# Attention with its side work in other places: the order of TensorE, VectorE, ScalarE and the loads around it

## The chip, the core and the metric

One Trainium2 chip, one of its cores. A core has TensorE (PE, matmul; its weight loads are the profile's PEld), VectorE (DVE), ScalarE (ACT), GpSimd (POOL) and SyncE (SP), which here only issues DMAs. The engines run their own instruction lists in order and wait for each other by semaphores. The metric is the time of one execution of the whole program on the device, in microseconds; lower is better.

## The reference

A decoder layer in float32 with batch 8, 224 tokens, width 512. Three parts, each with a layernorm ahead and a residual behind:

```python
x = x + mamba(layernorm(x))             # selective state space; ends with y @ W_out
x = x + cross_attention(layernorm(x), ctx)
x = x + moe(layernorm(x))               # router, 2 of 4 experts

qh = (q @ Wq + bq)   # 16 heads of 32; k and v from ctx (750 tokens) likewise
attn = softmax(qh @ kh.T / sqrt(32));  out = (attn @ vh) @ Wo + bo
router_logits = gelu(x @ rW1 + rb1) @ rW2 + rb2
```

## The kernel before

The program has four stages, one behind the other: `mamba_in`, `state_space`, `attention` and `experts`. Only `attention` is touched. Its input `y_d` (the state space's result), the keys `kh_d`, `kl_d` (high and low part) and the values `v_d` lie in device memory. It also computes what stands directly around the attention: the last projection of the mamba part (`project`), both layernorms (w = 0 for the attention, w = 1 for the experts), the queries, the end projection, and the router's hidden layer and logits.

The loop `steps()` runs over iterations `it` from -1 to 9 and, in each, over 16 slots `sl`, one per head; s = 16 it + sl is the head step. In a slot TensorE computes the scores of one head of one batch in two halves of 112 query rows, `scores(s, 0)` and `scores(s, 1)`. Both halves use the same two PSUM banks, so each one waits until VectorE has taken the row maxima of the half before (`negative_max`, a reduction over 750 keys, `max_done`). So a slot has two gaps for TensorE: one behind `scores(s, 0)` and one behind `scores(s, 1)`. In the first it computes the transposed scores of head s-3 (`turned_scores`), whose exponentials ScalarE then takes (`exponentials`) and GpSimd sums (`row_sum`). Every fourth slot has `values` (the product with v) and the next one `row_sums`, which waits for GpSimd's sums of four heads; every second slot has `turn_max`, which transposes the maxima for ScalarE's `turned_max`.

All other matmuls are side work. Iteration `it` prepares batch a = it+1 (project, layernorm w = 0, queries), finishes batch c = it-1 (end projection, layernorm w = 1, router's hidden layer) and has the logits of batch it-2. Slots 0 to 3 have one half of a projection each, slot 4 the logits, 5 and 6 the end projections, 8 both transposed norms, 9 to 12 the queries and the hidden layer, and 13 to 15 the rest of it. The whole order is written out by hand, in one loop per engine.

GpSimd's `with_bias(a)` in slot 10 writes x + bo into the buffer `xb[:, a % 2]`. It waits until the output of batch a-2 = c has been stored from the same buffer:

```python
if b >= 2:
    pool.wait_ge(x2_stored, 16 * (b - 1))
```

Next behind it in GpSimd's list stands the `row_sum` of that slot. SyncE stores that output in slot 8. It issues every DMA of the stage, all on one queue: keys for four heads in every slot with sl % 4 == 2, values in every slot with sl % 4 == 0, and the queries, which go to device memory and come back for a whole batch (`store_queries`, `load_queries`).

Iteration -1 has no head step: it is a prelude that only prepares batch 0. Iterations 8 and 9 drain the stage.

Of the kernel before, what the change touches and what calls it, by code (L numbers as in the profile page):

```python
# [13 lines left out]
P = 128  # L14
# [828 lines left out]
def attention(nc, x, kh_d, kl_d, v_d, y_d, W_out, Wq, bq, bv, Wo, bo, rW1, rb1, rW2, rb2, ident_in,  # L843
# [4 lines left out]

    ctx = ExitStack()
# [7 lines left out]
    with ctx:  # L857
# [3 lines left out]
        def sem(name):  # L861
# [29 lines left out]
        first_loaded, w_loaded, rest_loaded, g_loaded, x_loaded, q_loaded = (  # L891
            sem(n) for n in ("first_loaded", "w_loaded", "rest_loaded", "g_loaded", "x_loaded", "q_loaded"))
# [12 lines left out]
        N_W, N_REST = 4, 6  # L905
# [16 lines left out]
        def _(sp):  # L922
# [51 lines left out]
            load_g(1)  # L974
            for dst, src in ((bor[:], bo.partition_broadcast(P)), (wo[:], rows(Wo)), (rb1c[:], rb1), (rw1[:], rows(rW1)),
                             (rw2[:], rows(rW2)), (rb2r[:], rb2.partition_broadcast(P))):
                sp.dma_start(dst, src).then_inc(rest_loaded, 16)
            for j in range(KC):
                load_values(j)
            for it, sl, s in steps():  # L980
# [5 lines left out]
                if sl == 4 and it >= 0 and among(a + 1, B):  # L986
# [6 lines left out]
                if 9 <= sl < 9 + KC and among(a, B):  # L993
                    store_queries(a, sl - 9)
                if sl == 13 and among(a, B):
                    load_queries(a)
                    if a == 0:
                        load_keys(1)
                    if a + 1 < B:
                        load_x(a + 1)  # L1000
# [7 lines left out]
        def _(pool):  # L1008
# [15 lines left out]
            def with_bias(b):  # L1024
                if b == 0:
                    pool.wait_ge(rest_loaded, 16 * N_REST)
# [14 lines left out]
        def _(dve):  # L1041
# [16 lines left out]
            def statistics(b, w):  # L1058
                rows, ready = (xt, x1_done) if w == 0 else (xb[:, b % 2], x2_done)
                for u in range(2):  # L1060
                    dve.wait_ge(ready, 2 * b + u + 1)
                    nc.vector.bn_stats(st[:, 2 * w + u], rows[:, u]).then_inc(stat[w], 1)
# [6 lines left out]
            def normalise(b, w):  # L1069
                rows = xt if w == 0 else xb[:, b % 2]  # L1070
                dve.wait_ge(std[w], b + 1)
                nc.vector.reciprocal(rstd[:, w], rstd[:, w]).then_inc(rstd_done[w], 1)
                dve.wait_ge(rstd_done[w], b + 1)
                if b >= 1:
                    dve.wait_ge(xn_mm[w], 2 * b)
                    if w == 1:
                        dve.wait_ge(xn_stored, 16 * b)
                for u in range(2):
                    nc.vector.tensor_scalar(xn[w][:, u], rows[:, u], mv[:, 2 * w + u, 0:1], rstd[:, w, u:u + 1],
                                            ALU.subtract, ALU.mult).then_inc(xn_done[w], 1)  # L1080
# [9 lines left out]
            def hidden(b, q, bank):  # L1090
# [3 lines left out]
                nc.vector.tensor_scalar(rh[:, q], ps[:, bank, 0:L], rb1c[:, q:q + 1], None, ALU.add).then_inc(rh_pre, 1)  # L1094
# [5 lines left out]

            def outputs(J):
                b, j = J // KC, J % KC
                dve.wait_ge(sums_mm, J + 1)
                nc.vector.reciprocal(rinv[:], ps[:, PV_BANK, L:2 * L]).then_inc(rinv_done, 1)
                dve.wait_ge(rinv_done, J + 1)
# [12 lines left out]
            for it, sl, s in steps():  # L1118
                a, c, last = it + 1, it - 1, it - 2
                if it == 0 and sl == 0:  # L1120
                    dve.wait_ge(rest_loaded, 16 * N_REST)
                if among(s, STEPS):
                    negative_max(s, 0)
                if among(a, B):
                    if sl in (1, 3):
                        residual1(a, sl // 2)
                    if sl == 4:
                        statistics(a, 0)
                    if sl == 7:
                        normalise(a, 0)  # L1130
                    if 9 <= sl < 9 + KC:
                        low_queries(a, sl - 9)
                if sl == 4 and among(last, B):
                    logits(last)
                if among(c, B):
                    if sl in (5, 6):
                        residual2(c, sl - 5)
                    if sl == 6:
                        statistics(c, 1)
                    if sl == 7:  # L1140
                        normalise(c, 1)
                    if sl in (13, 14, 15):
                        hidden(c, {13: 4, 14: 6, 15: 7}[sl], BANK6)
                if among(s, STEPS):
                    negative_max(s, 1)
                if (s - SUM_LAG) % 4 == 0 and among((s - SUM_LAG) // 4, B * KC):
                    outputs((s - SUM_LAG) // 4)
                if among(c, B) and 9 <= sl < 14:
                    hidden(c, {9: 0, 10: 1, 11: 2, 12: 3, 13: 5}[sl], BANK5)

        @block.scalar
        def _(act):
# [19 lines left out]
            def turned_norm(b, w, u):  # L1172
                act.wait_ge(xn_mm[w], 2 * b + u + 1)
                nc.scalar.activation(xnT[w][:, :, u * TT:(u + 1) * TT],
                                     ps[:, (BANK6, BANK5)[u], 0:KC * TT].rearrange("p (k t) -> p k t", k=KC),
# [18 lines left out]
            for it, sl, s in steps():  # L1194
# [5 lines left out]
                if sl == 7:  # L1200
# [4 lines left out]
                if sl == 8:  # L1205
                    for w, b in ((0, a), (1, c)):
                        if among(b, B):
                            for u in range(2):
                                turned_norm(b, w, u)
                if 9 <= sl < 9 + KC and among(a, B):  # L1210
                    high_queries(a, sl - 9)
                if s % 2 == 0 and among((s - 2) // 2, STEPS // 2):
                    turned_max((s - 2) // 2)

        @block.tensor
        def _(pe):
# [60 lines left out]
            def project(b, u, half):  # L1277

                if half == 0:
# [6 lines left out]
                for c in range(4 * half, 4 * half + 4):  # L1286
                    ins = nc.tensor.matmul(ps[0:TT, (BANK5, BANK6)[u]], gT[:, c, u * TT:(u + 1) * TT], wout[:, c],
                                           start=(c == 0), stop=(c == CC - 1))
                if half == 1:
                    ins.then_inc(out_mm, 1)  # L1290

            def turn_norm(b, w, u):
                pe.wait_ge(xn_done[w], 2 * b + u + 1)
                if w == 0:
                    if b >= 2:
                        pe.wait_ge(x2_done, 2 * batches(b - 1))
                else:
                    pe.wait_ge(xn_turned[0], 2 * batches(b + 3))
                for k in range(KC):
                    ins = nc.tensor.transpose(ps[:, (BANK6, BANK5)[u], k * TT:(k + 1) * TT], xn[w][:, u, k * P:(k + 1) * P],  # L1300
# [3 lines left out]
            def queries(b, j):  # L1304
                if j == 0:
# [3 lines left out]
                    if b >= 2:  # L1309
                        pe.wait_ge(xn_turned[1], 2 * batches(b - 1))  # L1310
# [7 lines left out]
            def end_project(b, u):  # L1318
                if u == 0:
# [4 lines left out]
                elif b >= 1:  # L1324
                    pe.wait_ge(lg_done, 2 * batches(b))
                for j in range(KC):
                    ins = nc.tensor.matmul(ps[0:TT, (BANK6, BANK5)[u]], oT[:, j, u * TT:(u + 1) * TT], wo[:, j],
                                           start=(j == 0), stop=(j == KC - 1))
                ins.then_inc(wo_mm, 1)

            def hidden(b, q, bank):
                if q == 0:
                    pe.wait_ge(xn_turned[1], 2 * b + 2)
                elif q == 4:
# [539 lines left out]
```

## Time and profile before

| | us |
|---|---|
| median of 3 runs (lowest, highest) | 2938.28 (2930.95, 2944.82) |
| profiled execution, time / span | 2944.2 / 2942.5 |
| busy share of the span: PE, DVE, ACT, POOL | 85%, 49%, 41%, 44% |
| mean granted TensorE clock | 0.915 of full |
| attention: first DMA issue of the stage | 1078.6 |
| attention: first scores (iteration 0, slot 0) | 1153.57 |
| attention: iteration 1, slot 0 / iteration 7, slot 0 | 1241.26 / 1870.49 |
| attention: first DMA issue of the experts | 2021.65 |

Times of the trace count from the start of the span. The page cuts the span in 40 slices of 73.6 us each, and the attention fills slices 15 to 27:

```profile
PE   5998569999999974788988988883589989999991
PEclk9998779999999997799989999886799999999996
```

Each digit is a share in tenths: of busy time for PE, of full speed for PEclk, the clock that TensorE was granted. Nowhere in the attention's middle does PE reach the 99 of the neighbouring stages.

### The profile page before, as it was taken

How to read it: one execution, taken by the hardware profiler on the slowest of the kernel's cores; microseconds unless marked ns; L12 is line 12 of the kernel's file. 1: busy time of each engine (PE TensorE's matmuls, PEld its weight loads, DVE VectorE, ACT ScalarE, POOL GpSimd, SP SyncE). 2: the span in 40 equal slices, each digit the busy share in tenths (PEclk: the TensorE clock that was granted, in tenths of full speed). 3: DMA queues.
4: the chain of work that ended last, by engine and by line, in shares of the span. 5: the costliest groups of instructions: out<-in, count | busy, mean ns of one | idle time of the engine just before them, and what ended most of it. 6: DMA issues, size and time to landing. Idle time of an engine off the chain costs nothing. (4 is left out here: it accounts for less than half of the span.)

```text
span 2942.5 us, 39312 instructions
## 1 busy us (share of the span) xinstructions
PE 2491.5 (85%) x14320; PEld 2017.7 (69%) x14320; DVE 1430.8 (49%) x1880; ACT 1206.3 (41%) x2611; POOL 1297.2 (44%) x892
## 2 busy tenths in 40 slices
PE   5998569999999974788988988883589989999991
PEld 4984358888888862555665665652478888888881
DVE  5342479999999961455554454443021212121213
ACT  2333367777777621333433333332233333333330
POOL 3321247777777740544544544542563090009004
PEclk9998779999999997799989999886799999999996
DMA  9323765555565445434434452415531031002015
GB/s 290 126 105 95 222 192 170 164 160 157 175 172 175 133 137 133 114 93 104 113 95 94 106 119 70 108 29 187 179 107 57 29 122 42 15 29 79 29 64 157
DMA packets 257561, 349.20 MB, mean 119 GB/s; under 512 B 36574, under 2 KB 183966, under 8 KB 256270
## 3 DMA queue, kind: packets, MB, share of 16 engines
q1 hardware_dynamic: 235790, 281.32, 34.5%
q0 software_dynamic: 16256, 55.85, 5.7%
q10 hardware_dynamic: 5376, 10.23, 0.9%
q8 instruction: 81, 1.33, 0.2%
q14 instruction: 58, 0.48, 0.1%
HBM read 215.97 MB, written 131.35 MB: 118 GB/s over the span
## 5 line engine op out<-in xcount | busy, mean ns | idle before, releaser
L655 POOL TENSOR_TENSOR s_hc<-s_h,s_Cc 128x896 f32<-128x896 f32 x256 | 494.9, 1938 | 206.7 <-DVE s_h L760 102.4
L760 DVE TENSOR_TENSOR_SCAN s_h<-s_decay,s_ub 128x928 f32<-128x928 f32 x256 | 527.6, 2080 | 11.1 <-ACT s_decay L690 2.7
L798 PE MATMUL s_yps<-s_hc,s_ident 128*128 128x224 f32 x2048 | 431.1, 354 | 1.1 <-POOL s_hc L655 1.1
L1016 POOL TENSOR_TENSOR t_part<-t_pT 125x672 f32<-125x672 f32 x128 | 206.0, 1609 | 437.4 <-ACT t_pT L1159 437.0
L690 ACT ACTIVATE s_decay<-s_dt,s_A 128x224 f32<-128x224 f32 x1024 | 388.0, 470 | 18.4 <-DVE s_h L760 18.3
L1698 DVE TENSOR_TENSOR e_hl<-e_ps,e_hh 128x256 fp32r<-128x256 f32 x256 | 108.7, 425 | 573.0 <-ACT e_ps L1744 573.0
L798 PEld LDWEIGHTS s_yps<-s_hc,s_ident 128*128 128x128 f32 x2048 | 369.3, 191 | 2.0 <-POOL s_hc L655 1.4
L1046 DVE TENSOR_REDUCE t_nmax<-t_ps 112x1 f32<-112x752 f32 x256 | 239.8, 937 | 184.7 <-PE t_ps L1227 184.3
L1770 PE MATMUL e_ps<-e_xTh,e_w1h 128*128 128x256 f32 x1024 | 293.3, 286 | 23.5 <-DVE e_xTl L1690 23.5
L1159 ACT ACTIVATE t_pT<-t_ps 125x448 f32<-125x448 f32 x384 | 181.2, 545 | 317.8 <-PE t_ps L1251 306.5
L1743 ACT ACTIVATE e_hh<-e_ps,e_b 128x256 fp32r<-128x256 f32 x256 | 121.8, 476 | 421.9 <-PE e_ps L1772 421.7
L1771 PE MATMUL e_ps<-e_xTl,e_w1h 128*128 128x256 f32 x1024 | 292.9, 286 | 0.0
L1772 PE MATMUL e_ps<-e_xTh,e_w1l 128*128 128x256 f32 x1024 | 289.9, 283 | 0.0
L1227 PE MATMUL t_ps<-t_k,t_q 96*112 96x376 f32 x512 | 182.4, 440 | 104.8 <-DVE t_nmax L1046 78.9
L787 PE MATMUL s_ub<-s_diag,s_ut 96*128 96x224 f32 (+2 forms) x1024 | 232.3, 350 | 36.4 <-DVE s_diag L724 22.9
L787 PEld LDWEIGHTS s_ub<-s_diag,s_ut 96*128 96x128 f32 x1024 | 157.9, 194 | 107.0 <-issue 54.5
L1770 PEld LDWEIGHTS e_ps<-e_xTh,e_w1h 128*128 128x128 f32 x1024 | 197.2, 193 | 34.5 <-issue 24.6
L1770 PE MATMUL e_ps<-e_w2h,e_hh 128*128 128x512 f32 x512 | 205.1, 400 | 10.9 <-DVE e_hl L1698 10.9
L1568 POOL TENSOR_TENSOR e_w1h<-e_stage,e_one 128x2048 fp32r<-128x2048 f32 x12 | 43.3, 3607 | 386.0 <-PE e_ps L1772 385.8
L1771 PEld LDWEIGHTS e_ps<-e_xTl,e_w1h 128*128 128x128 f32 x1024 | 197.1, 192 | 9.2
L1772 PE MATMUL e_ps<-e_w2h,e_hl 128*128 128x512 f32 x512 | 201.6, 394 | 0.0
L1771 PE MATMUL e_ps<-e_w2l,e_hh 128*128 128x512 f32 x512 | 201.1, 393 | 0.0
(202 smaller groups left out, 4375.1 us busy)
## 6 DMA issues: line engine op xcount, KB each, us to landing
s_ut<-ut_d SPq DMA_DIRECT2D x192, 128.0 KB, 3.3
e_stage<-in_L_ffn_We POOLq DMA_DIRECT2D x24, 1024.0 KB, 5.6
t_k<-kh_d SPq DMA_DIRECT2D x64, 375.0 KB, 6.5
xs_d<-a_zero POOLq DMA_DIRECT2D x30, 512.0 KB, 12.5
s_Cc<-cs_d SPq DMA_DIRECT2D x8, 1792.0 KB, 9.6
kh_d<-s_kh SPq DMA_DIRECT2D x32, 375.0 KB, 2.7
kl_d<-s_kl SPq DMA_DIRECT2D x32, 375.0 KB, 2.8
v_d<-s_v SPq DMA_DIRECT2D x48, 250.0 KB
```

The costliest lines, as they stand in the source:

```text
L655: nc.gpsimd.tensor_tensor(hc[:, u % 2, k], h[:, u % 2, k, :, 2:SLOT], Cc[:, b % 2, k], ALU.mult).then_inc(hc_done, 1)
L690: ins = nc.scalar.activation(decay[:, u % 2, :, n, 2:SLOT], dts[:, u % 2].rearrange("p (s t) -> p s t", s=NSEG), ACT.Exp, scale=A[:, u % C ...
L760: nc.vector.tensor_tensor_scan(h[:, u % 2, k].rearrange("p n t -> p (n t)"), decay[:, u % 2, k].rearrange("p n t -> p (n t)"), ub[:, s % 2 ...
L787: ins = nc.tensor.matmul(at[:, first:end, half * FA:half * FA + width], ut[:, u // 2 % 2, 2 * k + half, u % 2 * P:u % 2 * P + P], diag[:, ...
L798: ins = nc.tensor.matmul(yps[:, u % 2, 0:L], ident[:], hc[:, u % 2, :, n], start=(n == 0), stop=(n == NS - 1))
L1016: nc.gpsimd.tensor_tensor(part[:], p[:, 0:3], p[:, 3:6], ALU.add).then_inc(sum_step, 1)
L1046: nc.vector.tensor_reduce(nmax[:, u, h:h + 1], ps[0:TT, 0:2, 0:EVEN], AX.XY, ALU.max, negate=True).then_inc(max_done, 1)
L1159: nc.scalar.activation(pT[:, g % PT, 2 * i:2 * i + 2], ps[0:CT, TURN_BANK + i, 0:2 * L].rearrange("p (i t) -> p i t", i=2), ACT.Exp).then_ ...
L1227: ins = nc.tensor.matmul(ps[0:TT, i, 0:EVEN], q3[0:ROWS3, b % 2, h, u * TT:(u + 1) * TT], k3[0:ROWS3, J % 2, h % 4, i * (CTX - EVEN):i * ( ...
L1770: nc.tensor.matmul(out, sh, mh, start=first, stop=False)
L1771: nc.tensor.matmul(out, sh, ml, start=False, stop=False)
L1772: return nc.tensor.matmul(out, sl, mh, start=False, stop=last)
```

## The change

TensorE's side work is cut into smaller pieces that stand in both gaps of a slot: a projection in quarters, the logits and the end projections in halves, the transposed norms by 112 tokens. The queries run two to a slot in 8 and 9. The transposes of one norm now share one bank, and the hidden layer alternates between two banks. `turn_max` stands directly behind `scores(s, 1)`. On VectorE the reciprocal of the sums is cut in two (`inverse_sums`) and `outputs` moves to the next slot; statistics, `variance` and `normalise` are split; most of the side work stands behind the second maximum. ScalarE takes the square root of the first norm in slot 6 and that of the second in slot 9, where both stood in slot 7. On SyncE the stores and loads of the queries move to slots 8 to 10, and the store of batch c's output from slot 8 to slot 10, behind the loads of the queries. The next values, `g` and the end weights are loaded behind the first queries, and TensorE and VectorE wait for the end weights in iteration 1 instead of 0.

```diff
             load_keys(0)
-            load_g(1)
-            for dst, src in ((bor[:], bo.partition_broadcast(P)), (wo[:], rows(Wo)), (rb1c[:], rb1), (rw1[:], rows(rW1)),
-                             (rw2[:], rows(rW2)), (rb2r[:], rb2.partition_broadcast(P))):
-                sp.dma_start(dst, src).then_inc(rest_loaded, 16)
-            for j in range(KC):
-                load_values(j)
+            sp.dma_start(bor[:], bo.partition_broadcast(P)).then_inc(bo_loaded, 16)
...
-                if sl == 8 and among(c, B):
+                if sl in (8, 9) and among(a, B):
+                    for j in (2 * sl - 16, 2 * sl - 15):
+                        store_queries(a, j)
+                if sl == 10 and among(a, B):
+                    load_queries(a)
+                if sl == 10 and among(c, B):
                     sp.wait_ge(x2_done, 2 * c + 2)
                     sp.dma_start(x2_d[c], xb[:, c % 2]).then_inc(x2_stored, 16)
...
-                if sl == 13 and among(a, B):
-                    load_queries(a)
...
+                if it == -1 and sl == 10:
+                    load_keys(1)
+                    load_g(1)
+                    for j in range(KC):
+                        load_values(j)
+                if sl == 11 and among(a + 1, B):
+                    load_x(a + 1)
+                if it == -1 and sl == 11:
+                    for dst, src in ((wo[:], rows(Wo)), (rb1c[:], rb1), (rw1[:], rows(rW1)), (rw2[:], rows(rW2)),
+                                     (rb2r[:], rb2.partition_broadcast(P))):
+                        sp.dma_start(dst, src).then_inc(rest_loaded, 16)
...
         @block.scalar
-                if sl == 7:
-                    if among(a, B):
-                        deviation(a, 0)
-                    if among(c, B):
-                        deviation(c, 1)
+                if sl == 6 and among(a, B):
+                    deviation(a, 0)
+                if sl == 9 and among(c, B):
+                    deviation(c, 1)
...
         @block.tensor
             def turn_norm(b, w, u):
                 pe.wait_ge(xn_done[w], 2 * b + u + 1)
+                if u == 1:
+                    pe.wait_ge(xn_turned[w], 2 * b + 1)
...
                 if among(s, STEPS):
                     scores(s, 0)
+                if sl in (8, 9) and among(a, B):
+                    queries(a, 2 * sl - 16)
                 if among(s - LAG, STEPS):
                     turned_scores(s - LAG)
...
                 if among(s, STEPS):
                     scores(s, 1)
+                if among(a, B):
+                    if sl == 7:
+                        turn_norm(a, 0, 1)
+                    if sl == 8:
+                        queries(a, 1)
+                if s % 2 == 0 and among((s - 2) // 2, STEPS // 2):
+                    turn_max((s - 2) // 2)
...
+                if among(a, B) and sl in (0, 1, 2, 4):
+                    project(a, sl // 2 if sl < 4 else 1, {0: 1, 1: 3, 2: 1, 4: 3}[sl])
```

SyncE's list in a middle iteration, slots 8 to 13, before: `x_d<-t_xb` is the store of batch c's output that GpSimd's `with_bias` waits for, `xn_d` its norm, `q_d` the queries' stores, `t_q` their loads, `t_k` keys, `t_v` values, `t_xt` the next x.

```order
L948 DMA t_v<-v_d 125x6x128
L990 DMA x_d<-t_xb 112x1024
L992 DMA xn_d<-t_xn 112x1024
L953 DMA q_d<-t_qh 128x224
L955 DMA q_d<-t_ql 128x224
L941 DMA t_k<-kh_d 32x4x750
L941 DMA t_k<-kl_d 32x4x750
L941 DMA t_k<-kh_d 32x4x750
```

After, from the last query store of the same iteration on:

```order
L958 DMA q_d<-t_ql 128x224
L944 DMA t_k<-kh_d 32x4x750
L944 DMA t_k<-kl_d 32x4x750
L944 DMA t_k<-kh_d 32x4x750
L966 DMA t_q<-q_d 32x16x224 x3
L993 DMA x_d<-t_xb 112x1024
L995 DMA xn_d<-t_xn 112x1024
L938 DMA t_xt<-in_x 112x2x512
```

The store of batch c's output stood ahead of the keys and of all the queries' DMAs; it now stands behind three loads of keys and three of queries.

TensorE's list in slots 8 and 9, before: `t_k,t_q` with 112x376 are the scores, `t_q,t_k` the transposed scores, `t_ident,t_xn` the transposed norms, `t_xnT,t_wq` a query matmul, `t_xnT,t_rw` a hidden one.

```order
L1227 MATMUL t_ps<-t_k,t_q 112x376 x2
L1251 MATMUL t_ps<-t_q,t_k 125x224 x6
L1300 MATMUL t_ps<-t_ident,t_xn 128x112 x8
L1227 MATMUL t_ps<-t_k,t_q 112x376 x2
L1273 MATMUL t_ps<-t_rsum,t_ones 32x224 x4
L1300 MATMUL t_ps<-t_ident,t_xn 128x112 x8
L1237 MATMUL t_ps<-t_ident,t_nmax 2x112 x2
L1227 MATMUL t_ps<-t_k,t_q 112x376 x2
L1251 MATMUL t_ps<-t_q,t_k 125x224 x6
L1314 MATMUL t_ps<-t_xnT,t_wq 128x224 x4
L1227 MATMUL t_ps<-t_k,t_q 112x376 x2
L1339 MATMUL t_ps<-t_xnT,t_rw 128x224 x4
```

After:

```order
L1273 MATMUL t_ps<-t_k,t_q 112x376 x2
L1358 MATMUL t_ps<-t_xnT,t_wq 128x224 x4
L1297 MATMUL t_ps<-t_q,t_k 125x224 x6
L1273 MATMUL t_ps<-t_k,t_q 112x376 x2
L1358 MATMUL t_ps<-t_xnT,t_wq 128x224 x4
L1283 MATMUL t_ps<-t_ident,t_nmax 2x112 x2
L1319 MATMUL t_ps<-t_rsum,t_ones 32x224 x4
L1273 MATMUL t_ps<-t_k,t_q 112x376 x2
L1358 MATMUL t_ps<-t_xnT,t_wq 128x224 x4
L1297 MATMUL t_ps<-t_q,t_k 125x224 x6
L1273 MATMUL t_ps<-t_k,t_q 112x376 x2
L1346 MATMUL t_ps<-t_ident,t_xn 128x112 x4
```

The first and the third query now stand ahead of the transposed scores of their slot, and the second norm's transposes moved from slot 8 to slots 9 and 10.

ScalarE's list, after, from the exponentials of slot 8 to those of slot 10; `t_pT` are the exponentials, `t_qh` a query's high part, `t_rstd` the square root of a norm, `t_xnT` a copy of transposed norms, `t_q` the maxima's copy.

```order
L1199 ACTIVATE t_pT<-t_ps 125x448 x3
L1224 ACTIVATE t_qh<-t_ps,t_bqc 128x224
L1205 ACTIVATE t_q<-t_ps 2x448
L1224 ACTIVATE t_qh<-t_ps,t_bqc 128x224
L1199 ACTIVATE t_pT<-t_ps 125x448 x3
L1210 ACT_TABLE_LOAD
L1210 ACTIVATE t_rstd<-t_rstd 112x2
L1224 ACTIVATE t_qh<-t_ps,t_bqc 128x224 x2
L1214 ACTIVATE t_xnT<-t_ps 128x4x112
L1199 ACT_TABLE_LOAD
```

The high part of each query stands behind three exponentials, and in slot 9 behind a table load and a square root as well, which before stood in slot 7.

## Rows read from the trace of the kernel before

**Rows 1.** Busy times by window: iterations 1 to 6, then the prelude.

```profile
1241.30:1870.50 629.20, 555.48 (x3617) 383.35 (x3617) 316.03 (x466) 221.95 (x423) 296.33 (x300) 0.92 0.44 101
...
1078.50:1153.50 75.00, 29.19 (x72) 16.55 (x72) 14.74 (x19) 6.37 (x10) 2.61 (x3) 0.67 0.68 190
```

**Rows 2.** Waits in the attention, 1153 to 1956: total us, times, longest.

```profile
PE t_ps L1227 <- DVE t_nmax L1046: 78.9, 81, 3.3
```

**Rows 3.** Timeline, TensorE, slots 2 to 4 of iteration 3: start, us, instructions.

```profile
1462.84 0.60 PE L1227 MATMUL t_ps<-t_k,t_q 96*112 96x376 f32 x2 [1.35 <-DVE t_nmax L1046]
1463.27 0.81 PE L1251 MATMUL t_ps<-t_q,t_k 98*125 98x224 f32 x6
1463.92 3.60 PE L1287 MATMUL t_ps<-t_wout,t_gT 128*112 128x512 f32 x8
1466.96 0.91 PE L1227 MATMUL t_ps<-t_k,t_q 96*112 96x376 f32 x2
1467.80 0.55 PE L1237 MATMUL t_ps<-t_ident,t_nmax 112*2 112x112 f32 x4
...
1473.86 2.48 PE L1264 MATMUL t_ps<-t_pT,t_v 125*32 125x224 f32 x48
...
1477.36 3.22 PE L1348 MATMUL t_ps<-t_rw,t_rh 128*112 128x4 f32 x32
```

**Rows 4.** The same, score starts of slot 7 and of slot 8.

```profile
1500.02 0.60 PE L1227 MATMUL t_ps<-t_k,t_q 96*112 96x376 f32 x2 [2.49 <-DVE t_nmax L1046]
...
1501.65 0.60 PE L1227 MATMUL t_ps<-t_k,t_q 96*112 96x376 f32 x2 [0.38 <-DVE t_nmax L1046]
...
1507.99 0.57 PE L1227 MATMUL t_ps<-t_k,t_q 96*112 96x376 f32 x2 [3.33 <-DVE t_nmax L1046]
```

**Rows 5.** The same, a query matmul and the scores behind it, slot 11.

```profile
1528.50 1.68 PE L1314 MATMUL t_ps<-t_xnT,t_wq 128*128 128x224 f32 x8
1529.86 0.66 PE L1227 MATMUL t_ps<-t_k,t_q 96*112 96x376 f32 x2
```

**Rows 6.** Timeline, ScalarE, slots 7 and 8 of iteration 3.

```profile
1502.38 1.28 ACT L1170 ACT_TABLE_LOAD   x1
...
1508.87 1.28 ACT L1159 ACT_TABLE_LOAD   x1 [4.90 <-PE t_ps L1251]
1510.17 1.42 ACT L1159 ACTIVATE t_pT<-t_ps 125x448 f32<-125x448 f32 x3
```

**Rows 7.** Groups by line, iterations 1 to 6: the reciprocal.

```profile
L1104 DVE RECIPROCAL t_rinv<-t_ps 128x224 f32<-128x224 f32 x24 | 37.2, 1550 | 0.0
```

**Rows 8.** Timeline, SyncE's issues in slots 12 to 14 of iteration 2.

```profile
1434.38 1.38 SPq L963 DMA_DIRECT2D t_q<-q_d  x3
...
1440.67 0.30 SPq L941 DMA_DIRECT2D t_k<-kh_d  x1
```

**Rows 9.** Timeline, TensorE: the first scores of iteration 3.

```profile
1450.27 0.57 PE L1227 MATMUL t_ps<-t_k,t_q 96*112 96x376 f32 x2 [1.19 <-issue]
```

**Rows 10.** DMA issues 1400 to 1452: times, KB each, median us to landing.

```profile
x_d<-t_xb SPq DMA_DIRECT2D x1, 448.0 KB, 6.8
```

**Rows 11.** Timeline, GpSimd, slot 10: with_bias, then one row_sum.

```profile
1521.20 2.50 POOL L1032 TENSOR_TENSOR t_xb<-t_xt,t_bor 112x512 f32<-112x512 f32 x2
1524.44 1.61 POOL L1016 TENSOR_TENSOR t_part<-t_pT 125x672 f32<-125x672 f32 x1 [0.74 <-ACT t_pT L1159]
...
1526.87 0.66 POOL L1022 TENSOR_TENSOR t_rsum<-t_part 125x224 f32<-125x224 f32 x1
```

**Rows 12.** Timeline, prelude: values' loads, queries' loads, first scores.

```profile
1116.15 12.59 SPq L948 DMA_DIRECT2D t_v<-v_d  x4
...
1144.19 1.38 SPq L963 DMA_DIRECT2D t_q<-q_d  x3
...
1153.57 0.94 PE L1227 MATMUL t_ps<-t_k,t_q 96*112 96x376 f32 x2 [12.11 <-issue]
```

**Rows 13.** Timeline, TensorE, the drain: hidden matmuls.

```profile
2000.29 1.78 PE L1339 MATMUL t_ps<-t_xnT,t_rw 128*128 128x224 f32 x8 [0.55 <-DVE t_rh L1094]
```

More of the change, by code:

```diff
@@ L1123, in _ @@
                     negative_max(s, 0)
+                if combine and sl != 9:
+                    outputs(J)
+                if combine and sl == 9:
+                    inverse_sums(J, 1)
                 if among(a, B):
[L1125 to L1128, printed above, removed]
-                    if sl == 7:
-                        normalise(a, 0)
-                    if 9 <= sl < 9 + KC:
-                        low_queries(a, sl - 9)
@@ L1133, in _ @@
-                if sl == 4 and among(last, B):
-                    logits(last)
-                if among(c, B):
[L1136 to L1143, printed above, removed]
+                    if sl == 2:
+                        residual1(a, 0)
@@ L1144, in _ @@
+                if sl == 9 and among(a, B):
+                    low_queries(a, 2)
                 if among(s, STEPS):
                     negative_max(s, 1)
[L1146 to L1149, printed above, removed]
+                if inverse:
+                    inverse_sums(J, 0)
+                    if sl != 8:
+                        inverse_sums(J, 1)
@@ new lines, in _ @@
+                if combine and sl == 9:
+                    outputs(J)
+                if sl == 5 and among(last, B):
+                    logits(last)
+                if among(a, B):
+                    if sl == 2:
+                        statistics(a, 0, 0)
+                    if sl == 5:
+                        statistics(a, 0, 1)
+                        variance(a, 0)
+                if among(c, B):
+                    if sl in (6, 7):
+                        residual2(c, sl - 6)
+                    if sl == 7:
+                        statistics(c, 1, 0)
+                    if sl == 8:
+                        variance(c, 1)
+                    if sl == 9:
+                        normalise(c, 1, 1)
+                    if 11 <= sl < 15:
+                        hidden(c, {11: 1, 12: 2, 13: 4, 14: 6}[sl])
@@ L1275, in row_sums, with project @@
                 ins.then_inc(sums_mm, 1)
-            def project(b, u, half):
-                if half == 0:
+            def project(b, u, quarter):
+                if quarter == 0:
                     if u == 0:
@@ L1285, in project @@
                         pe.wait_ge(q_low, KC * b)
-                for c in range(4 * half, 4 * half + 4):
+                for c in range(2 * quarter, 2 * quarter + 2):
                     ins = nc.tensor.matmul(ps[0:TT, (BANK5, BANK6)[u]], gT[:, c, u * TT:(u + 1) * TT], wout[:, c],
                                            start=(c == 0), stop=(c == CC - 1))
-                if half == 1:
+                if quarter == 3:
                     ins.then_inc(out_mm, 1)
@@ L1354, in _ @@
                 a, c, last = it + 1, it - 1, it - 2
-                if it == 0 and sl == 0:
+                if it == 1 and sl == 0:
                     pe.wait_ge(rest_loaded, 16 * N_REST)
```

192 lines of the change are left out of this document (107 added, 85 removed).

## The prediction

> **What bounds the kernel now.** I first read the windows. From the first scores of iteration 1 (1241.3) to those of iteration 7 (1870.5) TensorE is busy 555.5 of 629.2 us, VectorE 316, ScalarE 222 and GpSimd 296, and the granted clock is 0.92 of full [rows 1]. So TensorE's list sets the pace: an iteration takes 629.2 / 6 = 104.9 us, of which (629.2 - 555.5) / 6 = 12.3 are idle. The waits name the idle time: 81 times a score matmul waited for VectorE's maximum, 78.9 us in the whole stage [rows 2]. The clock is the second loss. 0.92 means 1.2 GHz instead of 2.4 for 16% of the time, about 17 us in an iteration; about 5 of them are lost, since part of that time is waiting. Last comes the timeline, which shows how a gap works. With nothing but the transposed scores in it, the next scores start 1501.65 - 1500.02 = 1.63 us after the last ones: score, maximum, score again. That is the floor of a gap. Work that fits below it costs nothing, and the rest costs its own time [rows 4]. A slot is two such gaps.
>
> **The pieces at full clock.** Scores 0.43 (1462.84 to 1463.27), transposed scores 0.65 (to 1463.92), half a projection and the scores behind it 3.88 (to 1467.80), so the half 3.45 and a quarter 1.72; `turn_max` 0.5, `values` 2.4, the logits 3.1, so 1.55 per half [rows 3]. A query or a hidden piece takes 1.36 from its start to the next scores [rows 5]; with the score's longer tail I take 1.5. Row sums 0.4, an estimate: 8 of the 48 like instructions of `values`.
>
> **Slots 0 to 6.** After the change each is the larger of 1.63 and the sum of its pieces, twice. Slot 0: 0.43 + 0.65 + 1.72 = 2.8, and 0.43 + 0.5 + 0.4 + 1.72 = 3.05, so 5.85. In the same way slot 1 gives 4.95, 2 gives 5.45, 3 gives 5.65, 4 gives 5.7, 5 gives 6.5, 6 gives 5.6: 39.7 in all. VectorE keeps up: a maximum ends 1.6 after its scores, and gaps of 2.6 and more leave it over 1 us for a residual or the outputs. Now slots 0 to 6 of iteration 3 take 1500.02 - 1450.27 = 49.75 [rows 4, 9], part of it at low clock. This is the gain of the change: 8 to 10 us an iteration. Halving the reciprocal (1.55 [rows 7]) adds one instruction's start-up, 0.1, in VectorE's free time.
>
> **Slot 7.** Both transposes of the first norm now go through one bank, so the second waits until ScalarE has copied the first. ScalarE has three exponentials of 1.42 ahead of that, and a table load of 1.28, since the exponentials' load starts only when the transposed scores are there (1508.87, after 4.90 idle) [rows 6]. That is 0.93 + 1.28 + 1.42 + 0.55 = 4.2 after the slot's start, then 0.5 and values 2.4: 7.15. Before: 1507.99 - 1500.02 = 7.97 [rows 4].
>
> **Slots 8 and 9.** Here it gets worse. The low part of query 0 stands on VectorE between the two maxima of slot 8. It waits for the high part, which on ScalarE is behind exponentials that now start after the query. Scores 0.43, query 1.5, transposed scores and 0.5 to the first exponential, 1.42, high part 0.45, low part 0.45: 4.85 us, and only then does query 1 start on TensorE. With `turn_max` and row sums slot 8 is 7.25. In slot 9 query 2 waits for the low part of query 1 (2.05 into the slot), its transposed scores end at 4.2, the exponentials at 5.5, then table load 1.28, root 0.2, reciprocal and half a `normalise` 0.75, low part 0.45. TensorE's next scores have been done since 4.7, but transposes and query 3 wait until about 8, and slot 9 takes 9.9. Together 17.15, against 13 to 14 before. By the bounds, nothing of the ScalarE chain waits (10.4) or all of it does (18).
>
> What the rows show is a table load of 1.28 at each change between square root and exponential, one of each per iteration now [rows 6] and two of each after. The Trainium skill says the same in "ScalarE: Activation LUTs", section "Table sets: the hidden batching unit": batch activations by table set; it speaks against the split of the two roots. Its figure, 1283 ns, agrees with the trace.
>
> **Slots 10 to 12.** The first exponentials of slot 10 wait for ScalarE's queue and the table load, so `turn_max` and hidden piece 0 come late: about 5.95. The largest new wait follows. GpSimd's `with_bias` in slot 10 needs the store of batch c's output. Before, that store was issued in slot 8, two slots ahead. Now it is issued in slot 10, behind keys (1.15 MB) and queries (1.38 MB), with its own 0.46 MB: 2.99 MB. The trace shows the same bytes in one row of loads: queries issued at 1434.38, x behind them, keys at 1440.67 [rows 8], and the scores that need these keys at 1450.27 [rows 9]: 15.9 us. The keys' issue in slot 10 comes 1.6 after its start, so the store lands near 17. Then `with_bias` 2.5 and one `row_sum`, 1524.44 to 1527.53, 3.1 [rows 11]: 23 after the start of slot 10. That sum is the last that the row sums of slot 12 wait for. TensorE would reach them at 5.95 + 5.4 + 3.5 = 14.9, so it waits 8 us, with a hidden piece and all later scores behind it. Bounds: a store with a free path lands after 6.8 [rows 10], so a wait of 3 (issue at 5.5, 12.3, 17.9); with a slower queue, 11. I take 8, since the row with equal bytes is the nearest. Six iterations have it, 1 to 6; SyncE also waits there for `with_bias`, before it loads x, which nobody needs before slot 2.
>
> Slots 10 to 12 thus take 24.9, slots 13 to 15 4.7 + 5.1 + 5.0 (keys load in 8 us, just in time).
>
> **Sum of a middle iteration.** 39.7 + 7.15 + 17.15 + 24.9 + 14.8 = 103.7. The same way of summing comes out about 1.3 short of the hidden slots of before, so 105 at full clock. Idle stretches of 3 and 8 us remain, and where TensorE had idled 2.49 and 3.33 us it then ran at half clock (the clock is 0.92 on average [rows 1, 4]); I keep the 4 to 5 us that the clock costs now: 109, that is +4 on 104.9, +24 for six. Ends: 3 less per wait bound down to 5 less, and 3 more.
>
> **Prelude, first and last iterations.** SyncE spends 12.6 us in issuing the values before the queries' stores can leave [rows 12]; that goes, so the queries come back 11.5 earlier, at about 1142 instead of 1153.6. But `g` of batch 1 now stands behind queries and keys. 3.45 MB at 188 GB/s (2.99 MB in 15.9 us) is 18.3 us from 1132.7: TensorE waits in slot 0 for `project` until 1151. And x of batch 1, behind the values (5.44 MB in all), lands at about 1162 for VectorE in slot 2; the kernel now is there at about 1167, an estimate of two slots of 6 to 7 us behind its first scores. So 4 to 5 us stay, not 11.5: -5. Iteration 0 has no end work and is bound by maxima and the low clock: 0. Iteration 7 has no queries and no `with_bias`: -3. In the drain hidden pieces wait for the bias one by one, 0.55 + 0.45 us each [rows 13]; two banks hide that for five of eight: -4.
>
> **Total.** +24 - 5 - 3 - 4 = +12 on the profiled 2944.2: 2956. The profiled execution stands 5.9 above the median, so 2950 for a median.
>
> **Rivals.** (1) The store lands early, faster than before. Speaking for it: writes may overtake reads, as no row shows a store behind many loads. Then slot 12 waits 3 or less, 5 to 6 us less per iteration: 2950 - 33 = 2917. Against it: x behind the queries took its turn. The rule for it stands in the Trainium skill, "DMA: Bandwidth & Descriptors", section "Two DMAs through the same engine are not ordered": descriptors of one queue start in order but are pipelined, and reads and writes have separate queues. (2) The clock stays at 2.4 GHz: the pieces fill both gaps, and the logits, 3.1 us of 4-column matmuls ahead of slot 5's slow end projection, are split. Then the 5 us come back, with the waits as I have them: 2950 - 27 = 2923. Against it are the waits in slots 9 and 12. (3) On the other side, slower: the same wait in slot 12 starts another stretch of 1.2 GHz each time. Slots 13 to 15 and the next slot 0, some 14 us of full work, then cost 3 to 5 more, 2950 + 25 = 2975. It decides if the clock falls behind that wait as it does behind the 3.33 us ahead of slot 8. (4) Nothing of the prelude's gain stays: 2955.
>
> **Chances.** Forecast 0.45, with 2936 to 2964 as its own range; (1) 0.18; (2) 0.1; (3) 0.22; (4) 0.05. Within 0.5% of 2938.3 is 2923.6 to 2953.0, about what a measurement can tell from no change. Faster: most of (1) and half of (2), 0.23. Slower: (3), two fifths of the forecast: 0.39. Same 0.38. Range 2912 to 2976.
>
> **What would show it.** In the trace after: GpSimd's `t_xb` group waits for a DMA for 10 us or more in slot 10; score or sum matmuls wait for GpSimd's `t_rsum` in slot 12, 6 to 8 us; slots 0 to 6 below 42 us; slot 9 near 10 us, with VectorE waiting for ScalarE; 14 square root table loads instead of 8 between the first and the last scores; first scores near 1142 and a wait for `g` right behind. It is wrong if slot 12 shows no wait, or if the clock in the middle is above 0.95.

## The result, and the profile after

The changed kernel takes 2966.05 us (median of 4 runs, 2963.61 to 2969.68) against 2937.73 for the kernel before (4 runs). The ratio is 1.0097, 95% interval 1.0071 to 1.0123: 28 us slower. In the profiled executions the span grows by 21.7 us, from 2942.5 to 2964.2.

The windows of the profile after cover the prelude with iteration 0, iterations 1 to 6, iteration 7, and the drain. The columns are those of [rows 1]: start and end, length, busy time and instructions of TensorE, its weight loads, VectorE, ScalarE and GpSimd, the granted clock, the DMA engines' share, and GB/s.

```profile
1078.50:1138.60 60.10, 26.21 (x72) 14.27 (x72) 15.23 (x19) 6.37 (x10) 2.61 (x3) 0.77 0.55 144
1138.60:1242.00 103.40, 75.63 (x402) 47.23 (x402) 41.65 (x54) 28.83 (x56) 40.53 (x41) 0.75 0.58 144
1242.00:1899.40 657.40, 543.40 (x3621) 384.89 (x3617) 310.08 (x490) 236.47 (x435) 295.84 (x299) 0.92 0.41 97
1899.40:1978.30 78.90, 69.60 (x483) 51.24 (x479) 44.80 (x65) 33.50 (x61) 44.44 (x47) 0.85 0.27 66
```

Iterations 1 to 6 take 657.4 us instead of 629.2 [rows 1], 109.6 each instead of 104.9. TensorE is busy for less time than before, 543.4 against 555.5, so the loss is all waiting: 114 us idle instead of 74. Iteration 1 starts at 1242.0 against 1241.3, so the earlier first scores (1138.7 against 1153.6 [rows 12]) brought nothing. Iteration 7 is 2.8 us shorter, and so is the drain.

By slots, as means of iterations 1 to 6 from score start to score start, the change wins in slots 0 to 6 and loses more than that in slots 7 to 12:

| slots | before, us | after, us |
|---|---|---|
| 0 to 6 | 50.2 | 39.8 |
| 7 to 9 | 20.4 | 27.2 |
| 10 to 12 | 18.1 | 27.9 |
| 13 to 15 | 16.1 | 14.7 |
| iteration | 104.9 | 109.6 |

These are waits of the profile after in the whole stage. The third answers to [rows 2]; the others have no counterpart of that size before.

```profile
POOL t_xb L1038 <- DMA x_d<-t_xb: 124.8, 6, 22.2
...
PE t_ps L1319 <- POOL t_rsum L1028: 51.7, 6, 9.3
...
PE t_ps L1273 <- DVE t_nmax L1052: 28.0, 47, 4.8
...
PE t_ps L1346 <- DVE t_xn L1086: 22.8, 7, 3.5
...
PE t_ps L1358 <- DVE t_ql L1094: 20.3, 15, 1.6
```

The side work in pieces did its part: waits for the maxima fall from 78.9 us to 28.0. In their place GpSimd waits six times for the store of batch c's output, 20.8 us each, and TensorE six times for GpSimd's sums, 8.6 us each. The last two rows are the second loss, in slots 8 and 9: TensorE waits for the second norm (`t_xn`) and for the low parts of the queries (`t_ql`). The timeline of iteration 3 shows how the first two hang together:

```profile
1524.44 0.67 PE L1273 MATMUL t_ps<-t_k,t_q 96*112 96x376 f32 x2
...
1526.13 0.45 SPq L944 DMA_DIRECT2D t_k<-kh_d  x1
...
1529.17 0.74 SPq L993 DMA_DIRECT2D x_d<-t_xb  x1
...
1542.64 2.48 POOL L1038 TENSOR_TENSOR t_xb<-t_xt,t_bor 112x512 f32<-112x512 f32 x2 [19.55 <-DMA x_d<-t_xb]
...
1548.20 0.98 PE L1319 MATMUL t_ps<-t_rsum,t_ones 125*32 125x224 f32 x8 [8.73 <-POOL t_rsum L1028]
```

Slot 10 starts at 1524.44, the keys are issued 1.7 later and the store 4.7 later. It lands 13.3 us after its issue instead of 6.8 [rows 10], `with_bias` starts 18.2 into the slot, and TensorE, which has nothing else ahead of the row sums of slot 12, waits 8.73. That slot took 14.4 to 16.6 us in the six iterations, against 5.8 before.

The second loss is largest in slot 9, where ScalarE stands between TensorE and VectorE:

```profile
1518.46 1.42 ACT L1199 ACTIVATE t_pT<-t_ps 125x448 f32<-125x448 f32 x3 [3.12 <-PE t_ps L1297]
...
1519.90 1.28 ACT L1210 ACT_TABLE_LOAD   x1
...
1521.19 0.20 ACT L1210 ACTIVATE t_rstd<-t_rstd 112x2 f32<-112x2 f32 x1
1521.30 0.43 ACT L1224 ACTIVATE t_qh<-t_ps,t_bqc 128x224 fp32r<-128x224 f32 x1
1521.43 0.17 DVE L1080 RECIPROCAL t_rstd<-t_rstd 112x2 f32<-112x2 f32 x1 [3.52 <-ACT t_rstd L1210]
...
1522.63 0.60 PE L1346 MATMUL t_ps<-t_ident,t_xn 112*128 112x112 f32 x4 [3.50 <-DVE t_xn L1086]
```

Three exponentials, a table load, the root, the reciprocal, `normalise`, and only then TensorE, idle for 3.50 us.

### The profile page after: what moved, and what is told of

Same layout as the page of the kernel before. It is cut to its first block and busy times, and to the rows that moved or that the text cites. A ratio compares the mean times of both kernels' runs of the same rounds, so it can differ in the third digit from the quotient of the medians.

```text
span 2964.2 us, 39345 instructions
## 1 busy us (share of the span) xinstructions
PE 2479.2 (84%) x14320; PEld 2018.7 (68%) x14320; DVE 1426.5 (48%) x1912; ACT 1221.4 (41%) x2623; POOL 1298.9 (44%) x892
## 5 line engine op out<-in xcount | busy, mean ns | idle before, releaser
L690 ACT ACTIVATE s_decay<-s_dt,s_A 128x224 f32<-128x224 f32 x1024 | 388.0, 470 | 18.3 <-DVE s_h L760 18.2
L1273 PE MATMUL t_ps<-t_k,t_q 96*112 96x376 f32 x512 | 189.7, 454 | 40.5 <-DVE t_nmax L1052 28.0
```

The lines of the kernel that those rows point to most:

```text
L690: ins = nc.scalar.activation(decay[:, u % 2, :, n, 2:SLOT], dts[:, u % 2].rearrange("p (s t) -> p s t", s=NSEG), ACT.Exp, scale=A[:, u % C ...
L1273: ins = nc.tensor.matmul(ps[0:TT, i, 0:EVEN], q3[0:ROWS3, b % 2, h, u * TT:(u + 1) * TT], k3[0:ROWS3, J % 2, h % 4, i * (CTX - EVEN):i * ( ...
```

## The experiments

Each was timed in rounds with the kernel before on the same chip. The cuts below show the lines that matter; an added line that the changed kernel has elsewhere is moved from there. Medians of the kernel before differ between chips, from 2938 to 2947, so the ratio to it is the number to compare.

**The store back in slot 8** (e1_store8). The changed kernel, with

```diff
+                if sl == 8 and among(c, B):
+                    sp.wait_ge(x2_done, 2 * c + 2)
+                    sp.dma_start(x2_d[c], xb[:, c % 2]).then_inc(x2_stored, 16)
                 if sl in (8, 9) and among(a, B):
                     for j in (2 * sl - 16, 2 * sl - 15):
...
                 if sl == 10 and among(c, B):
-                    sp.wait_ge(x2_done, 2 * c + 2)
-                    sp.dma_start(x2_d[c], xb[:, c % 2]).then_inc(x2_stored, 16)
```

> The changed kernel with one DMA moved back: the store of batch c's output (x_d<-t_xb) stands in slot 8, ahead of the queries' stores, not in slot 10 behind keys and queries. Theory (the store's place is what costs): GpSimd's with_bias no longer waits, slot 12 falls from 16 us to 6, six iterations give back 60 us, 2906 us (2895 to 2916), that is faster than the kernel before. Rival (ScalarE's chain in slots 7 to 10 and the low clock are the loss, and the wait in slot 12 only hides it): a new wait takes most of it and the time stays above 2940.

Measured: 2908.48, ratio 0.9874 (0.9847 to 0.9901). Iterations 1 to 6 take 600.1 us, slot 12 takes 5.36, and the wait for `t_rsum` is gone. GpSimd's `with_bias` now waits 2.0 us at most, for `normalise`. The place of one DMA is worth 2.2%: with the store in slot 10 the change is 1.0% slower than the kernel before, with it in slot 8 it is 1.3% faster.

**The consumer moved instead** (e2_bias13), the store still late:

```diff
-                if sl == 11 and among(a + 1, B):
+                if sl == (11 if it < 0 else 14) and among(a + 1, B):
                     load_x(a + 1)
...
-                if sl == 10 and among(it + 1, B):
+                if sl == (10 if it < 0 else 13) and among(it + 1, B):
                     with_bias(it + 1)
```

> The changed kernel with the store left in slot 10, but with_bias on GpSimd moved from slot 10 to slot 13 (and the next x load from slot 11 to slot 14), from iteration 0 on. It takes away what stands behind the wait, not the late store. Theory: what costs is that row_sum stands behind with_bias on GpSimd, so this gives the same as moving the store, 2900 to 2920 us, slot 12 at 6 us. Rival (the queue itself, with 3 MB in a row in slot 10, holds up keys or something else): it stays above 2940.

Measured: 2922.75, ratio 0.9932 (0.9907 to 0.9957), 2914.5 in the profiled execution. The store still lands 13.4 us after its issue (median), but `with_bias` waits only 4.3 us in all, and slot 12 takes 5.36. So the wait in slot 12 does not come from the late store by itself, but from `row_sum` queued behind its waiter. The median came out 3 us above the range; the profiled execution was the fastest of the eight, so no trace shows that part. It does show where this place costs more than the store in slot 8 (iterations 1 to 6 take 609.6 us against 600.0): slot 13 rose from 4.4 to 6.2 in four of the iterations. In just these four VectorE's `outputs` ran beside the moved `with_bias` and took 2.4 us instead of 0.34, and TensorE waited for the VectorE step behind it:

```profile
1427.01 2.53 POOL L1038 TENSOR_TENSOR t_xb<-t_xt,t_bor 112x512 f32<-112x512 f32 x2
...
1428.87 2.37 DVE L1120 TENSOR_SCALAR t_oT<-t_o,t_bvc 128x224 f32<-128x224 f32 x1
...
1431.65 1.78 PE L1384 MATMUL t_ps<-t_xnT,t_rw 128*128 128x224 f32 x8 [1.57 <-DVE t_rh L1101]
```

That the one slows the other is not tested here.

**The same wait put into the kernel before** (e11_before_store12): its store moved from slot 8 to slot 12.

```diff
-                if sl == 8 and among(c, B):
+                if sl == 12 and among(c, B):
                     sp.wait_ge(x2_done, 2 * c + 2)
                     sp.dma_start(x2_d[c], xb[:, c % 2]).then_inc(x2_stored, 16)
+                if sl == 8 and among(c, B):
                     sp.wait_ge(xn_done[1], 2 * c + 2)
```

> The kernel before with one DMA moved: the store of batch c's output from slot 8 to slot 12. Theory (the wait of with_bias holds up row_sum and so TensorE's row sums, whatever the order of the rest): the store lands about 7 us into slot 12, with_bias and one row_sum take 5.6, TensorE wants the sums 3 us into slot 12, so it waits about 9 us in each of six iterations: 54 us more than the kernel before, 2992 us (2980 to 3010). Rival (the wait in the changed kernel comes from its packed queue): under 10 us more.

Measured: 3001.12 beside 2946.74, ratio 1.0161 (1.0125 to 1.0196). Two of its waits:

```profile
POOL t_xb L1033 <- issue: 110.8, 6, 19.3
...
PE t_ps L1274 <- POOL t_rsum L1023: 52.0, 6, 9.3
```

For the first the profile names no releaser, but it ends with the store's landing: in iteration 2 the store is issued at 1440.97 and lands 6.6 later, and `with_bias` starts at 1447.70. The waits are those of the changed kernel (51.7 us for the sums there), in another order of work and with a store that lands after 7.2 us (median). The packed queue only makes the lateness; the rest is the wait with `row_sum` behind it.

**The loads of the prelude alone, in the kernel before** (e3_loads):

```diff
                     if a == 0:
                         load_keys(1)
+                        load_g(1)
+                        for j in range(KC):
+                            load_values(j)
                     if a + 1 < B:
                         load_x(a + 1)
+                    if a == 0:
+                        for dst, src in ((wo[:], rows(Wo)), ...
```

> The kernel before with only the loads of the prelude in the new order: g, values and end weights behind the first queries, end weights waited for in iteration 1. Theory (the wait moves from the queries to g in slot 0 and x in slot 2): the first scores start 11 to 15 us earlier, but iteration 1 starts at the same time within 3 us; 2934 us (2930 to 2940). Rival (the earlier queries are worth their 11 us): 2926 or less.

Measured: 2950.34 beside 2941.13, ratio 1.0020 (0.9996 to 1.0043). The time lies above my range: the 4 us of gain that I expected are not there, and neither are the 11 us of the rival. Its timeline in iteration 0:

```profile
1138.72 0.97 PE L1229 MATMUL t_ps<-t_k,t_q 96*112 96x376 f32 x2 [12.42 <-DMA t_q<-q_d]
...
1146.60 6.32 PE L1289 MATMUL t_ps<-t_wout,t_gT 128*112 128x512 f32 x8 [6.92 <-DMA t_gT<-y_d]
...
1165.35 0.69 DVE L1053 TENSOR_TENSOR t_xt<-t_ps,t_xt 112x512 f32<-112x512 f32 x1 [9.46 <-DMA t_xt<-in_x]
...
1166.94 0.97 PE L1229 MATMUL t_ps<-t_k,t_q 96*112 96x376 f32 x2 [8.24 <-DVE t_nmax L1048]
```

The first scores come 14.9 us earlier, then 6.92 are lost to `g` and 8.24 of TensorE's time to x, and iteration 1 starts at 1244.4 instead of 1241.3.

**g ahead of the queries, x ahead of the values** (e4_gx), in the changed kernel:

```diff
             sp.dma_start(bor[:], bo.partition_broadcast(P)).then_inc(bo_loaded, 16)
+            load_g(1)
...
                     load_keys(1)
-                    load_g(1)
+                    load_x(1)
                     for j in range(KC):
                         load_values(j)
```

> The changed kernel with g of batch 1 loaded ahead of the queries again and x of batch 1 ahead of the values. Theory: TensorE's wait of 6.9 us for g in slot 0 of iteration 0 and VectorE's of 6.7 us for x in slot 2 (4.8 us on TensorE) go; 10 us less than the changed kernel, 2956 us. Rival (the queue is full anyway, and the time is only moved on to the queries' own loads): no difference, 2963 to 2968.

Measured: 2948.10, ratio 1.0012 (0.9995 to 1.0029), 18 us below the changed kernel where I expected 10. The queries' loads were issued 0.6 us earlier than in the changed kernel, so they paid nothing for `g`. Iteration 0 shrank from 103.3 to 88.2 us and iteration 1 starts at 1226.2: 15.8 us earlier, of which the two waits are 11.7. TensorE's busy time in iteration 0 fell by 2.6 us as well (73.05 against 75.63), with a granted clock of 0.79 instead of 0.75.

**High parts ahead of the exponentials** (e5_high): e1_store8, in slots 8 and 9, with

```diff
+                if sl in (8, 9) and among(a, B):
+                    high_queries(a, 2 * sl - 16)
                 if among(s - LAG, STEPS):
                     exponentials(s - LAG)
```

> The changed kernel with the store back in slot 8 (e1_store8) and, in slots 8 and 9, the high part of queries 0 and 2 ahead of the exponentials in ScalarE's list. Theory (three exponentials of 1.42 us stand between a query and its high part): slot 8 falls from 7.3 us to about 5.9 and slot 9 by up to 1, 15 us less than e1_store8, 2893 us. Rival (slots 7 to 10 wait for the roots' table loads, not for the exponentials): slot 8 falls but slot 9 grows, within 5 us of e1_store8.

Measured: 2889.07, ratio 0.9809 (0.9785 to 0.9833). Slot 8 fell from a mean of 7.8 us to 5.7, as expected, which is 12.6 us in six iterations. Slot 9 didn't gain but rose from 11.3 to 11.6, so that half of the rival is right. Slot 10 fell from 7.1 to 6.2 (5.6 us), which I had not in the sum: 19 us in all.

**Both roots left out** (e7_noroot): e1_store8 with `ACT.Copy` for `ACT.Sqrt` in `deviation`, which leaves the square root out of both norms.

```diff
-                nc.scalar.activation(rstd[:, w], rstd[:, w], ACT.Sqrt).then_inc(std[w], 1)
+                nc.scalar.activation(rstd[:, w], rstd[:, w], ACT.Copy).then_inc(std[w], 1)
```

> e1_store8 with both square roots of the attention stage left out (a copy in their place), so without their table loads and without the exponentials' reloads behind them. Its output differs from the reference's in the norms. Theory: a root's load in slot 9 and a reload in slot 10 lie on the path, and a reload in slot 7: about 1.3 us each, 3.9 in each of six iterations, 23 us less than e1_store8, 2885 us. Rival (ScalarE is 35% busy, and the loads hide as its share says): under 6 us.

Measured: 2877.17, ratio 0.9767 (0.9742 to 0.9793), 31 us less than e1_store8, 5 in each iteration, where I expected 23. Four loads are gone in each iteration: those of the two roots and those of the exponentials behind them. Slot 7 fell from a mean of 9.05 to 6.05, slot 10 from 7.1 to 4.7, slot 6 from 6.3 to 5.5, but slot 9 only from 11.3 to 10.3. So the loads are worth more than I said, but mostly in slots 7 and 10, and slot 9 has another cause left. What still stands ahead of its root are the exponentials, with or without a load; e9_rootfirst tests that.

**The three together** (e6_best): the edits of e1_store8, e4_gx and e5_high.

```diff
+            load_g(1)
...
+                if sl == 8 and among(c, B):
+                    sp.wait_ge(x2_done, 2 * c + 2)
...
+                    load_x(1)
...
+                if sl in (8, 9) and among(a, B):
+                    high_queries(a, 2 * sl - 16)
```

> The changed kernel with the store in slot 8, g ahead of the queries and x ahead of the values in the prelude, and the high parts ahead of the exponentials. If the three parts add up: 2966 - 58 - 18 - 15 = 2875 us. Rival (they overlap, or the low clock takes a part back): 2885 or more.

Measured: 2870.06, ratio 0.9744 (0.9720 to 0.9769). They add up: 5 us below the 2875 expected.

**The roots first as well** (e9_rootfirst): in slots 6 and 9 `deviation` moves ahead of the exponentials, and ahead of the high part.

```diff
+                if sl == 6 and among(a, B):
+                    deviation(a, 0)
+                if sl == 9 and among(c, B):
+                    deviation(c, 1)
                 if sl in (8, 9) and among(a, B):
                     high_queries(a, 2 * sl - 16)
                 if among(s - LAG, STEPS):
                     exponentials(s - LAG)
```

> As e6_best, and the square roots of slots 6 and 9 also stand ahead of the exponentials of their slot, so that their table load falls where ScalarE waits for TensorE, and the reload stands ahead of exponentials in slots 6 and 9 and not in 7 and 10. Theory: normalise starts 2 us earlier in slot 9, and slots 7 and 10 lose the reload: 15 to 25 us less than e6_best, about 2855 us. Rival: the exponentials of slot 9 come 2.6 us later and hold up the transposed maxima in slot 10, no gain.

Measured: 2808.69, ratio 0.9543 (0.9520 to 0.9566): 61 us less than e6_best where I expected 15 to 25, and 4.6% faster than the kernel before. It has the same number of table loads in the stage, 45. In slot 9 of iteration 3, seen on ScalarE, VectorE and TensorE:

```profile
1534.58 1.28 ACT L1212 ACT_TABLE_LOAD   x1
...
1535.88 0.20 ACT L1212 ACTIVATE t_rstd<-t_rstd 112x2 f32<-112x2 f32 x1
...
1537.24 0.55 DVE L1088 TENSOR_SCALAR t_xn<-t_xb,t_mv,t_rstd 112x512 f32<-112x512 f32 x1
...
1537.90 1.28 ACT L1201 ACT_TABLE_LOAD   x1
...
1538.24 0.55 PE L1348 MATMUL t_ps<-t_ident,t_xn 112*128 112x112 f32 x4
```

The load falls where ScalarE had nothing to do, and the transposes start without an idle time. Slot 9 takes 6.16 us instead of 11.6. Slots 6 and 7 together are 3.5 us shorter per iteration and slot 10 is 1.35 shorter; the two roots were not moved one at a time. The windows of iterations 1 to 6, first of e6_best, then of e9_rootfirst, tell where the rest came from:

```profile
1221.70:1802.30 580.60, 527.21 (x3621) 376.02 (x3617) 310.02 (x490) 236.43 (x435) 296.59 (x299) 0.95 0.47 110
```

```profile
1224.20:1743.00 518.80, 500.84 (x3621) 360.72 (x3617) 307.51 (x490) 235.81 (x435) 296.06 (x299) 1.00 0.52 123
```

Of the 61.8 us, 35.4 are idle time (53.4 to 18.0), and 26.4 are the same 3621 instructions in less time: the granted clock rose from 0.95 to 1.00, that is, the stretches at 1.2 GHz are gone. That mending slot 9 would also take the low clock away was not in my estimate.

**Only ScalarE's order mended, the store left late** (e10_root_only).

```diff
+                if sl == 6 and among(a, B):
+                    deviation(a, 0)
+                if sl == 9 and among(c, B):
+                    deviation(c, 1)
+                if sl in (8, 9) and among(a, B):
+                    high_queries(a, 2 * sl - 16)
                 if among(s - LAG, STEPS):
                     exponentials(s - LAG)
...
-                if sl == 9 and among(c, B):
-                    deviation(c, 1)
```

> The changed kernel with ScalarE's order alone mended (square roots and high parts ahead of the exponentials in slots 6, 8 and 9), the store of batch c's output still in slot 10 and the loads as the change has them. Theory (two separate losses): slots 6 to 9 fall from 33 to 23.5 us, slot 10 by 1.4, but slot 12 grows by that 1.4, since its wait hangs on the store in slot 10: about 59 us less than the changed kernel, 2907 us. Rival (the wait in slot 12 swallows whatever is gained ahead of it): 2950 or more.

Measured: 2894.70, ratio 0.9809 (0.9777 to 0.9841), 71 us below the changed kernel by medians and 2.9% by the ratios, more than the 59 us that I expected. Iterations 1 to 6 take 592.3 us instead of 657.4. Slots 6 to 9 take 23.5 and slot 12 rose from a mean of 15.9 to 17.1, both as expected. The two losses are separate, and taking away either of them turns the change from slower into faster.

## Why the prediction was right, and where it was off

**Direction and mechanism.** The measured 2966 lies within the range of 2912 to 2976, but 2 us above the forecast's own 2936 to 2964; the forecast of 2950 stood nearer to no change than to what came. Slower is the likeliest of its three outcomes, with a chance of 0.39 against 0.38 for no change. The two mechanisms named, the store behind keys and queries and ScalarE's chain in slots 7 to 9, are the ones that the experiments took away (e1, e2, e9, e10), and the first was also made anew (e11). The signs named came: 20.8 us of waiting for `with_bias`, 8.6 for the sums, slots 0 to 6 at 39.8, slot 9 at 9.8 to 11.5, 14 root loads between the first and the last scores instead of 8, and a wait for `g` right behind the first scores.

**Slots 0 to 6.** Forecast 39.7; iteration 3 has 39.65. Adding pieces gap by gap, with the floor of 1.63, gave the sum to 0.1 us. Single slots were off by up to 0.7 (slot 6: 5.6 forecast, 6.27 measured), so that closeness is in part errors that cancel.

**Slot 7.** Forecast 7.15, measured 8.6 to 8.8. The second transposes started 4.22 us into the slot in all six iterations, as forecast (4.2). What was longer is the work behind that wait, at half clock: `values` and the rest took 3.5 to 4.1 us instead of 2.4. In iteration 3, whose slot 7 runs from 1498.50 to 1507.31:

```profile
1502.72 0.57 PE L1346 MATMUL t_ps<-t_ident,t_xn 112*128 112x112 f32 x4 [1.71 <-ACT t_xnT L1214]
1503.22 4.16 PE L1310 MATMUL t_ps<-t_pT,t_v 125*32 125x224 f32 x48
```

The one slot 7 of e5_high whose `values` ran at full clock took 7.12. Without the reload in it the slot takes 6.05 (e7_noroot) and 6.15 (e9_rootfirst).

**Slots 8 and 9.** Forecast 17.15, measured 17.1 to 20.3, mean 18.5. The low end is the forecast; the high ones, iterations 4 and 6, have half clock there (0.82 and 0.80 of full in slots 8 and 9 of iteration 4, 1.00 in both in iteration 3).

**Slots 10 to 12.** Forecast 24.9, measured 27.3 to 28.4. The wait itself was well sized (8 against 8.73), the start of `with_bias` at 18.2 instead of 17. Its TensorE work ran at half clock around the wait: the hidden piece behind it took 2.92 us instead of 1.68. The sum had the clock as one lump of 4 to 5 us per iteration, and the whole came out at 109 against 109.6 measured: +28 for six iterations instead of +24. That it is so close is in part luck. In e9_rootfirst the same 3621 matmul instructions ran with the clock at 1.00 and were busy for 500.8 us, in the changed kernel for 543.4: the clock cost 7.1 us per iteration, not 4. By that measure some 102.5 are left where the sum had 105, so the clock was 3 too small and the rest 2.5 too large.

**Prelude and iteration 0.** This is the term that was wrong: -5 forecast, +0.7 measured. The landings were near (g 1151 forecast, 1146.6 measured; x 1162 and 1165.5), and so were the first scores (1142 and 1138.7). What failed was the step "Iteration 0 has no end work and is bound by maxima and the low clock: 0". Behind the two waits the gain was still there as forecast: the scores of slot 3 start at 1167.06 against 1172.23. But iteration 0 has the queries of batch 1 in slots 8 and 9 like every other, and these two slots took 14.4 us instead of 8.2; slots 3 to 7 lost 3.6 more, in a window that runs at 0.75 of the clock instead of 0.81. Behind them the changed kernel is 4.7 us late, and it is 0.8 late at iteration 1, where the kernel before waits 3.8 us itself. So ScalarE's chain, which the sum of a middle iteration has, was put at nothing here. Rival (4) came true. Iteration 7 (-2.8) and the drain (-2.8, forecast -4) were near.

**Sum.** +12 forecast, +23.2 in the stage by the profile, and 1.5 back outside it. Of the 11 us between them about 6 are the prelude with iteration 0, 4 the middle iterations and 1 the drain. The medians differ by 28.3, 6.6 more than the spans. The profiled execution of the kernel before took 2944.2, 6.5 above its median, so the two profiles understate the difference by about that.

**Rivals.** (1), an early landing: refuted, 13.3 us. (2), a clock that stays up: not in the changed kernel, 0.92 as before, though it is what e9_rootfirst then showed. (3), more low clock behind the wait: slots 13 to 15 took 14.1 to 15.3 us against 14.8 forecast, so hardly there; it was in slot 12 itself. Its time, 2975, is nearer to the measured 2966 than the forecast is, but not for its reason.

**Table loads and queues.** The Trainium skill says in "ScalarE: Activation LUTs", section "Table sets: the hidden batching unit", to batch activations by table set. That is only half of this case. Leaving out all four loads of an iteration gave 5 us per iteration (e7_noroot, against e1_store8); keeping all of them and moving the roots ahead of the exponentials gave 10 (e9_rootfirst, against e6_best). The separate queues for reads and writes of which the Trainium skill tells ("DMA: Bandwidth & Descriptors", section "Two DMAs through the same engine are not ordered") gave the store no way past the loads here: it landed 16.4 us after the first keys' issue in iteration 3, against 15.9 forecast.

## What to carry to other kernels

When work is moved, write down for every wait what is queued behind the waiter on its engine; here a DMA two slots later cost 55 to 58 us (e11, e1) through an add that nobody needs soon. An engine that is a third busy, as ScalarE here, can still be the bound: put short links of a chain (a root, a high part) ahead of the bulk work in its list, and let table loads fall into its idle time. When a loop still idles a few us each round, look at the granted clock as a second loss: here 26 of the last 62 us won were the clock.

## What the runs showed of the hardware

Over iterations 1 to 6 the granted clock was 1.00 with TensorE idle for 18 of 519 us (e9_rootfirst), 0.95 with 53 of 581 (e6_best) and 0.92 with 114 of 657 (the changed kernel), for the same matmuls. The idle time alone does not give the clock: it was 0.95 with 77 of 592 (e10_root_only), and 0.92 with 74 of 629 in the kernel before.

A store of 0.46 MB landed 13.3 us after its issue behind 2.5 MB of loads on the same queue, against 6.8 to 7.2 behind one load of values (the kernel before, e1_store8, e11_before_store12).

A table load ahead of an ACTIVATE that itself waits for another engine ran at once, during the wait (in the drain of the changed kernel at 1993.7, with the root at 2015.6); the one ahead of exponentials ran only when the transposed scores were there (1508.87 [rows 6]). The ACTIVATE behind a load started 1.29 to 1.30 us after the load did (1519.90 and 1521.19, 1534.58 and 1535.88).

VectorE's `outputs`, 0.34 us otherwise, took 2.4 us in the four places of e2_bias13 where it ran beside GpSimd's `with_bias`.
